# Attention output projection from 16-bit parts, maxima as bias of exponentials per head, normalisation on GpSimd

## What is computed

```python
def _L0_gnn_ref(x, batch, edge_index, edge_attr, Wq, bq, Wk, bk, Wv, bv, Wo, bo, We, be, num_graphs):
    ...
    q = (x @ Wq + bq).reshape(num_graphs, n, H, hd)
    k = (x @ Wk + bk).reshape(num_graphs, n, H, hd)
    v = (x @ Wv + bv).reshape(num_graphs, n, H, hd)
    attn = jnp.einsum('bnhd,bmhd->bnmh', q, k) * scale
    eb = edge_attr @ We + be
    ...
    attn = attn.at[b_idx, loc_src, loc_dst].add(eb)
    attn = jax.nn.softmax(attn, axis=2)
    out = jnp.einsum('bnmh,bmhd->bnhd', attn, v).reshape(n_total, hid)
    return out @ Wo + bo
```

## Time and profile before

| | us |
|---|---|
| median of 3 runs | 1372.05 |
| lowest, highest | 1370.95, 1372.5 |
| profiled execution, its time | 1371.25 |
| its span, first to last instruction | 1369.7 |

### The profile page before, as it was taken

One profiled execution on the slowest core, in us unless ns is written; L12 is line 12 of the kernel. 1 busy time (PEld: TensorE's weight loads), 2 busy tenths in 40 slices (PEclk: granted clock), 3 DMA queues, 4 the chain that ended last, 5 costly groups with the idle time before them and its releaser, 6 DMA issues.

```text
span 1369.7 us, 26459 instructions
## 1 busy us (share of the span) xinstructions
PE 1329.6 (97%) x11088; PEld 822.8 (60%) x11088; DVE 907.8 (66%) x1370; ACT 633.8 (46%) x1073; POOL 86.9 (6%) x79
## 2 busy tenths in 40 slices
PE   8889999989998999999999999999999999999998
PEld 8788899889997665444444444444444445344443
DVE  7898998999997887788768766432354223522423
ACT  2676666556655447863366434211262224422322
POOL 3120010011001120000000001011100000000000
PEclk9899999999999999999999999999999999999999
DMA  9633444344438651100000002032220323463201
GB/s 333 238 111 123 146 151 135 120 131 138 151 132 284 195 196 71 33 0 31 1 1 1 1 31 85 0 86 62 70 62 0 85 70 102 175 230 103 83 0 62
DMA packets 77813, 137.98 MB, mean 101 GB/s; under 512 B 18261, under 2 KB 30677, under 8 KB 76151
## 3 DMA queue, kind: packets, MB, share of 16 engines
q1 hardware_dynamic: 75022, 125.06, 27.8%
q0 software_dynamic: 1280, 5.77, 1.5%
q10 hardware_dynamic: 1384, 5.38, 1.1%
HBM read 82.85 MB, written 53.33 MB: 99 GB/s over the span
## 4 chain that ended last, share of the span: by engine, by line
PE 83%; DVE 11%; ACT 2%; issue 2%; DMA 1%; POOL 0%; ACTq 0%; DVEq 0%; SPq 0%; POOLq 0%
PE banks L2507 16%; PE banks L2446 14%; PE banks L2405 13%; PE banks L2557 12%; PE banks L1242 6%; PE banks L1658 4%; DVE x_sb L881 3%; PE banks L1179 3%; PE banks L1196 2%; PE banks L1253 2%; PE banks L1153 2%; DVE x_sb L864 1%; PE banks L2342 1%; PE banks L1628 1%; PE banks L1646 1%
## 5 line engine op out<-in xcount | busy, mean ns | idle before, releaser
L2507 PE MATMUL banks<-g,count 128*128 128x512 f16 x1024 | 227.1, 379 | 0.0
L2405 PE MATMUL banks<-w_parts,h_parts 128*128 128x512 f16 x960 | 215.8, 379 | 4.2 <-DVE h_parts L2645 2.4
L2507 PEld LDWEIGHTS banks<-g,count 128*128 128x128 f16 x1024 | 99.9, 98 | 113.2
L2557 PE MATMUL banks<-g,part 128*128 128x512 f16 x768 | 165.9, 379 | 0.0
L2405 PEld LDWEIGHTS banks<-w_parts,h_parts 128*128 128x128 f16 x960 | 90.7, 98 | 119.9 <-issue 9.7
L881 DVE TENSOR_TENSOR x_sb<-eb_parts,x_sb 128x4096 f16<-128x4096 f16 x64 | 145.8, 2278 | 0.0
L1242 PE MATMUL banks<-x_sb 128*128 128x128 f16 x2048 | 126.9, 221 | 11.8 <-DVE x_sb L881 11.8
L1242 PEld LDWEIGHTS banks<-x_sb 128*128 128x128 f16 x2048 | 120.9, 99 | 15.2 <-DVE x_sb L881 14.1
L2557 PEld LDWEIGHTS banks<-g,part 128*128 128x128 f16 x768 | 75.1, 98 | 90.6
L3010 DVE SCALAR_TENSOR_TENSOR part<-count,e_scale,part 128x1024 f16<-128x1024 f32 x29 | 37.2, 1284 | 105.9 <-ACT part L2292 105.9
L2292 ACT ACTIVATE part<-count,e_scale 128x1024 f16<-128x1024 f32 x29 | 33.3, 1148 | 110.9 <-PE banks L2557 110.9
(11 more groups left out here) (351 smaller groups left out, 2136.1 us busy)
## 6 DMA issues: line engine op xcount, KB each, us to landing
weight_dram<-w_new SPq DMA_DIRECT2D x60, 256.0 KB, 2.7
count<-weight_dram SPq DMA_DIRECT2D x29, 512.0 KB, 7.3
qk_dram<-stage SPq DMA_DIRECT2D x64, 128.0 KB, 3.0
tiles<-x_dram SPq DMA_DIRECT2D x32, 256.0 KB, 3.7
x_dram<-tiles SPq DMA_DIRECT2D x32, 256.0 KB, 2.8
count<-in_x SPq DMA_DIRECT2D x4, 1024.0 KB, 13.3
h<-in_x SPq DMA_DIRECT2D x16, 256.0 KB, 4.4
h_dram<-h_t SPq DMA_DIRECT2D x8, 512.0 KB, 2.9
```

What stands on the lines that cost most here:

```text
L2405: mm = pe.matmul(out, m.h_parts[:, slot, zh, k], m.w_parts[:, zw, k], start=n == 0 and layer != 3, stop=n == len(passes) - 1)
L2507: mm = pe.matmul(m.agg_ps[:, b], m.count[:, i, c, block], m.g[:, i, z], start=i == 0 and z == 0, stop=i == NT - 1 and z == 1)
L2557: mm = pe.matmul(m.banks[:, b], m.part[:, n % 3, z, b * P:(b + 1) * P], m.g[:, q, gz], start=q == 0 and (z, gz) == (0, 0), stop=q == NT - ...
```

## The change

Four things change, all in the attention stage.

1. The projection: the attention output is written as two f16 parts (high by ScalarE, low by VectorE), Wo is split into two f16 parts once at the start, and `output(t)` is twelve f16 matmuls (high by high, high by low, low by high) in place of four f32 ones. Powers of two scale the parts; `wo_undo` takes them out when VectorE adds the projection to x. The bias bv no longer goes in with the copy: bv times Wo is formed once and added to `bo_row`.
2. The maxima: VectorE forms the negated scores, takes their minimum per head, and subtracts nothing; ScalarE runs one exponential for each head, with the minimum as bias and scale -1.
3. The multiplication by the reciprocal and the copy of 64 columns go from VectorE to GpSimd, which also adds the bias row to x as before.
4. In `attention_act` the first copy of the attention output stands ahead of the exponentials of its period, in later periods behind them as before. SyncE waits for the last projection before it loads `dis_row`, whose place the parts of Wo now take.

```diff
@@ attention_pool
-    pool.wait_ge(s["in_bo"], 16)
+    def probabilities(t):
...
+        pool.wait_ge(s["summed"], t + 1)
+        pool.tensor_tensor(p3, p3, m.row_sum[:, t % 2].unsqueeze(2).to_broadcast([P, H, GN]), ALU.mult).then_inc(s["normal"], 1)
+        pool.wait_ge(s["normal"], t + 1)
+        pool.tensor_copy(prob[:, D:D + GN], prob[:, 0:GN]).then_inc(s["prob"], 1)
+    probabilities(0)
+    probabilities(1)
+    pool.wait_ge(s["wo_scaled"], 1)
     for t in range(NT):
-        pool.wait_ge(s[f"in_x{t // 2}"], 16)
-        pool.wait_ge(s["prob"], t + 1)
+        if t + 2 < NT:
+            probabilities(t + 2)
...
+        pool.wait_ge(s[f"in_x{t // 2}"], 16)
         pool.tensor_tensor(keep.x[:, t, :], keep.x[:, t, :], m.bo_row[:], ALU.add).then_inc(s["plus"], 1)
@@ attention_act
-        act.activation(prob, prob, ACT.Exp).then_inc(s["exped"], 1)
+        for hd in range(H):
+            part = prob[:, hd * GN:(hd + 1) * GN]
+            op = act.activation(part, part, ACT.Exp, bias=m.row_max[:, t % 2, hd:hd + 1], scale=-1.0)
+        op.then_inc(s["exped"], 1)
+
+    def wo_squares():
+
+        act.wait_ge(s["in_wo"], 16)
+        act.wait_ge(keep.first["chunk"], LAST)
+        act.activation(m.wo_unread[:], keep.wo[:], ACT.Square, accum_out=m.wo_square).then_inc(s["wo_squared"], 1)
+
+    def wo_high():
+
+        act.wait_ge(s["wo_scaled"], 1)
+        for k in range(KT):
+            act.activation(m.wo_parts[:, 0, k], keep.wo[:, k], ACT.Copy, scale=m.wo_scale).then_inc(s["wo_high"], 1)
...
-        for k in range(KT):
-            op = act.activation(m.att_t[:, k].rearrange("p (g n) -> p g n", g=2), m.av_ps[:, :, k * GN:(k + 1) * GN],
-                                ACT.Identity, bias=keep.bv_col[:, k:k + 1])
-        op.then_inc(s["copied_av"], 1)
+        for g in range(2):
+            act.activation(att_part(m, 0, g), av_half(m, g), ACT.Copy, scale=m.att_scale).then_inc(s["copied_av"], 1)
...
+        if t == FIRST:
+            wo_squares()
+        if t == -1:
+            copy_mixed(t + 1)
         if is_tile(t + 3):
             exponentials(t + 3)
+        if t == -2:
+            wo_high()
...
-        if is_tile(t + 1):
+        if is_tile(t + 1) and t >= 0:
             copy_mixed(t + 1)
@@ attention_pe
         if t:
-            pe.wait_ge(s["copied_av"], t)
+            pe.wait_ge(s["av_low"], 2 * t)
...
     def output(t):
-        pe.wait_ge(s["copied_av"], t + 1)
+        pe.wait_ge(s["copied_av"], 2 * t + 2)
...
         if t == 0:
-            pe.wait_ge(s["in_wo"], 16)
+            pe.wait_ge(s["wo_low"], KT)
+        for n, (za, zw) in enumerate(((0, 0), (0, 1), (1, 0))):
+            if za:
+                pe.wait_ge(s["av_low"], 2 * t + 2)
+            for k in range(KT):
+                mm = pe.matmul(m.wo_ps[:, t % 2], m.att_t[:, za, k, :], m.wo_parts[:, zw, k, :], start=n == k == 0, stop=za == 1 and k == KT - 1)
+        mm.then_inc(s["wo"], 1)
+
+    def wo_total():
+
+        pe.wait_ge(s["wo_squared"], 1)
+        pe.matmul(m.wo_ps[:, 0, 0:1], keep.one.to_broadcast([P, P]), m.wo_square, start=True, stop=True)
         for k in range(KT):
-            mm = pe.matmul(m.wo_ps[:, t % 2], m.att_t[:, k, :], keep.wo[:, k, :], start=k == 0, stop=k == KT - 1)
-        mm.then_inc(s["wo"], 1)
+            mm = pe.matmul(m.wo_ps[:, 1], keep.bv_col[:, k:k + 1].to_broadcast([P, P]), keep.wo[:, k], start=k == 0, stop=k == KT - 1)
+        mm.then_inc(s["wo_total"], 1)
...
             scores(t + 4)
+        if t == -3:
+            wo_total()
@@ attention_dve
-        dve.tensor_reduce(m.row_max[:, j], p3, axis=AX.X, op=ALU.max).then_inc(s["dve"], 1)
...
-        dve.tensor_tensor(p3, p3, m.row_max[:, j].unsqueeze(2).to_broadcast([P, H, GN]), ALU.subtract).then_inc(s["lowered"], 1)
+        dve.tensor_reduce(m.row_max[:, j], p3, axis=AX.X, op=ALU.min).then_inc(s["lowered"], 1)
...
-        dve.reciprocal(m.row_sum[:, j], m.row_sum[:, j]).then_inc(s["dve"], 1)
...
-        dve.tensor_tensor(p3, p3, m.row_sum[:, j].unsqueeze(2).to_broadcast([P, H, GN]), ALU.mult).then_inc(s["dve"], 1)
...
-        dve.tensor_copy(prob[:, D:D + GN], prob[:, 0:GN]).then_inc(s["prob"], 1)
+        dve.reciprocal(m.row_sum[:, j], m.row_sum[:, j]).then_inc(s["summed"], 1)
...
-        dve.tensor_tensor(keep.x[:, t, :], keep.x[:, t, :], m.wo_ps[:, t % 2], ALU.add).then_inc(s["wo_done"], 1)
+        dve.scalar_tensor_tensor(keep.x[:, t, :], m.wo_ps[:, t % 2], m.wo_undo, keep.x[:, t, :], ALU.mult, ALU.add).then_inc(s["wo_done"], 1)
...
+    def wo_powers():
...
+        dve.wait_ge(s["wo_total"], 1)
+        dve.wait_ge(s["in_bo"], 16)
+        dve.tensor_tensor(m.bo_row[:], m.bo_row[:], m.wo_ps[:, 1], ALU.add)
...
+    def wo_low():
+
+        for k in range(KT):
+            dve.wait_ge(s["wo_high"], k + 1)
+            dve.scalar_tensor_tensor(m.wo_parts[:, 1, k], keep.wo[:, k], m.wo_scale, m.wo_parts[:, 0, k], ALU.mult, ALU.subtract).then_inc(s["wo_low"], 1)
+
+    def att_low(t):
+
+        for g in range(2):
+            dve.wait_ge(s["copied_av"], 2 * t + g + 1)
+            dve.scalar_tensor_tensor(att_part(m, 1, g), av_half(m, g), m.att_scale, att_part(m, 0, g), ALU.mult, ALU.subtract).then_inc(s["av_low"], 1)
...
+        if t == -3:
+            wo_powers()
+        if t == -2:
+            wo_low()
         if is_tile(t - 1):
             op = add_out(t - 1)
+        if is_tile(t + 1):
+            att_low(t + 1)
```

48 lines of the change are left out of this document (36 added, 12 removed).

## The result

| | before | after |
|---|---|---|
| median (lowest to highest), us | 1370.95 (1366.69 to 1372.5), 7 runs | 1377.74 (1375.78 to 1378.4), 7 runs |
| ratio to before, 95% interval | | 1.0055 (1.0041 to 1.007) |
| profiled execution: time, span, granted clock | 1371.25, 1369.7, 0.989 | 1377.69, 1376.0, 0.986 |

The changed kernel is slower by 0.55%. In the listing after the change the lines are: L1580 exponentials, L1608 copy of the attention output, L1829 its low part, L1768 row sum, L1771 reciprocal, L1754 scores, L1758 minimum, L1777 output into x, L1555 and L1557 GpSimd's normalisation and wrapped copy, L1569 its addition, L1693 values, L1664 scores, L1675 transposes and L1708 projection on TensorE.

A forecast was written before the change was run, and what follows sets the result against it. The prediction took TensorE to set the pace before the change and a VectorE-ScalarE loop after it. Start + 9.6, twelve periods - 4.6, early periods - 1.2 and end + 1.6 gave + 5.4 us, so 1377, range 1371 to 1385.

The forecast's parts named there:

- TensorE alone at 5.24 to 5.27: Attention period: with twelve f16 projection matmuls TensorE by itself needs 5.24, with new waits 5.27 us, against 6.12 before.
- VectorE's work 4.9 to 5.0, GpSimd 2.9, ScalarE 3.65: Attention period: each engine's own work in us after the change, all under TensorE's 5.27.
- Exponentials at 0.235 each, 1.88 in all: ScalarE, each tile: eight 128x64 exponentials at 0.235 us from start to start, 1.88 us together.
- The loop of 5.74: Attention period: VectorE's and ScalarE's queues wait on each other in turn, making 5.74 us; 0.38 saved per tile.
- The start costs 9.6: Start of the attention stage: uncovered preparation delays the values of tile 1 from 442.04 to 451.7, 9.6 us lost.
- The end costs 1.6: End of the attention stage: low parts on full VectorE and GpSimd's longer way cost 1.6 us, between 0 and 2.5.
- The sum, + 5.4: Whole kernel: + 9.6 - 4.6 - 1.2 + 1.6 = + 5.4 us, giving 1377.
- TensorE stays the bound: Rival, attention period: exponentials of 1.4 us or less leave the loop at 5.27 or less; 1369 to 1372, chance 0.14.
- Upper end: Rival, attention period: exponentials of 2.4 to 2.8 us make the loop 6.3 to 6.6; 1385 to 1390, chance 0.11.
- Cheap preparation: Rival, stage start: VectorE's queue doesn't set it, so it costs 5 us; 1372 to 1373, chance 0.10.

The follow-up runs named there:

- e1: The changed kernel with ScalarE's copy of the attention output ahead of its exponentials in every period; 1375.34 us, ratio 1.0043 to the kernel before.
- e5: The changed kernel with the softmax taken back: one exponential, and the subtraction of the maximum on VectorE; 1387.22 us, ratio 1.0134 to the kernel before.
- e6: The changed kernel with sixteen exponentials of 32 columns in place of eight of 64; 1398.63 us, ratio 1.0219 to the kernel before.
- e11: The changed kernel with the normalisation and the wrapped copy back on VectorE; 1390.97 us, ratio 1.0158 to the kernel before.
- e2: The changed kernel with VectorE's powers waiting only for the sum of squares, bv times Wo signalled separately and added later; 1369.83 us, ratio 1.0005 to before.
- e3: The changed kernel with the edits of e1 and e2 together; 1369.06 us, ratio 0.9985 to the kernel before.
- e8: The kernel of e7 with VectorE's peak of the next layer's weights moved behind the row sum of tile 15; 1367.05 us, ratio 0.9979 to before.
- e4: The kernel before with eight exponentials whose bias is the minimum, and no subtraction; 1368.71 us, ratio 0.9992 to the kernel before.
- e7: The kernel of e3 with ScalarE's next-layer normalisations and first weight part ahead of the copy of tile 15; 1366.82 us, ratio 0.9979 to before.
- e12: The changed kernel with the edits of e5 and e11 together, leaving the 16-bit projection alone; 1389.49 us, ratio 1.0132 to the kernel before.

## Why the prediction was right

The forecast was 1377.0 and the median is 1377.74. The mechanism held: a loop through two queues in place of TensorE, and a start that costs more than the loop saves. That the number lies within 0.8 us is partly luck. The stage added 1.1 us less than the 5.4 forecast, 2.0 came from outside it (0.6 ahead and 1.4 behind), and the median of the kernel before, now of seven runs, is 1.1 lower than the one the sum began with. By its steps:

- *TensorE alone at 5.24 to 5.27.* Right. e1 has 5.27, with the projection at 2.75.
- *VectorE's work 4.9 to 5.0, GpSimd 2.9, ScalarE 3.65.* Near: VectorE is busy 10.00 of 12 us, 4.7 a period. GpSimd's multiplication took 1.04, not the 1.27 of the addition, so its period is 2.56. Costing GpSimd at nothing held in the even part for the changed kernel, and only there: what I didn't see is that GpSimd's longer work makes a VectorE operation with two SBUF inputs dear when the two fall together (e5). The change is spared this in its period because it takes both such operations away.
- *Exponentials at 0.235 each, 1.88 in all.* Measured 1.93 to the start of the copy, 0.24 each. The duration of one was 0.333. The Trainium skill's rule (ScalarE: Activation LUTs, What ACT_TABLE_LOAD costs) gives, as an estimate from its figures, 280 + 0.833 x 64 = 333 ns, and the trace agrees.
- *The loop of 5.74.* Right as a mechanism (e1, e6, e11) and 0.09 too long: most of it in the low part, 0.79 to the next start where I had 0.86. TensorE waits 0.21 before its projection by the bracket and 0.37 by starts (1.30 from the transposes to the projection, 0.93 in e1), where I had 0.4. The twelve periods saved 6.66 us and not 5.8. Three of them ran at 5.27, 5.27 and 5.36, as said.
- *The start costs 9.6.* Measured 9.45, but the cause named for it was half of the truth. I had the bias row end VectorE's wait and TensorE's product done long before, at 432.5. It took 5.19 us in place of 3.5, the first 3.1 of them at 1.2 GHz, and ended the wait at 435.06. The bias row, issued at 429.46 and landing some 5.4 us later, was there within 0.2 us of it. In e1 and e5 it was indeed the row that came last. In e5 the product, after the same 2.0 us of waiting, ran at full clock in 3.68 us, and the start was hardly shorter (28.35 against 28.68). So the two waits stood side by side, and taking away one alone gives little; e2 took VectorE's queue past both.
- *The end costs 1.6.* Measured + 1.85 to tile 15 and - 0.32 behind it. Which of the causes named there it was, the change's own trace doesn't separate. e3 shows the row sum of tile 15 behind the weight reduction as the gate once the loop is gone, and e8, which takes the reduction away from there, brings tile 13 to 15 down to 11.45, below the 11.83 of the kernel before.
- *The sum, + 5.4.* The stage gave + 4.3 and the span + 6.3. The 1.4 us behind the stage were in no step.
- *The rivals.* "TensorE stays the bound" needed exponentials of 1.4 us, which are 1.93. "Upper end" needed 2.4. "Cheap preparation" needed a start of 5 us.

Those 1.4 us go with the clock. The stretch behind the stage took 834.3 to 834.8 us in the traces of before, e1, e2, e3, e4 and e6, and 836.1 to 836.7 in those of after, e5 and e7 to e12. Each of the eight long ones has one stretch of 3.4 us at half clock, 299 to 300 us behind the second low part of the next layer, and none of the six short ones has any there. What stays open is why the clock falls there in some executions. Each kernel has one trace, so whether the after kernel does so in each execution isn't known.

## What to carry to other kernels

When work is moved between engines, write down the order in each queue and look for a ring: an engine that waits for a second, whose queue holds ahead of that answer something that waits for the first. Its length is the sum of the links, whatever each engine's busy share says, and reordering one queue can open it with no work added (e1), though what is moved ahead can hold something else, as the next layer's normalisations here until e7. And one-off preparation at the start of a stage deserves as much care as the loop: here a start that came 9.45 us later took more than the 6.7 us saved over twelve periods, and 6.2 of it was one wait that held two unrelated results. Four edits of order, with the same arithmetic, turned + 0.55% into - 0.53%.
